# Cross-attention with a gate: the step without a tile gets an x half of the gate and two q pieces, the columns of q are cut anew, and the opening and the last steps are written in another order

## The chip, the cores and the metric

The kernel runs on one core of a Trainium2 chip. The metric is the device time of one execution in microseconds, the median of several runs. TensorE (PE in the rows) does the matmuls, VectorE (DVE), ScalarE (ACT) and GpSimd (POOL) the elementwise work, and SyncE (SP) hands out all the DMA transfers.

## What is computed

For 32 batches of 112 rows x (512 wide) with a memory of 375 keys (256 wide), in float32:

```python
memory_proj = einsum('bme,de->bmd', memory, W_mem)
scores = einsum('bnd,bmd->bnm', x, memory_proj) / sqrt(512)
attn = softmax(scores)
memory_context = einsum('bnm,bmd->bnd', attn, memory_proj)
gate = sigmoid(einsum('bnf,df->bnd', concat([x, memory_context]), W_gate) + b_gate)
fused = x + gate * memory_context
out = fused * rsqrt(mean(fused**2) + 1e-6) * norm_w
```

The kernel reorders this: q = x W_mem (256 wide) is multiplied with the memory itself, and `am`, the mean of the memory under the softmax, is multiplied with W_mem and with the gate weights.

## The kernel before

**Precision.** Each operand of a matmul is split into a high and a low part (`_hi`, `_lo`, type fp32r); a product is three kinds of matmul: high x high, high x low, low x high. ACT writes the high part as a copy, DVE or POOL the low part as a difference. So each product needs an ACT copy and a difference ahead of it.

**Tiling.** Eight batches are a group of 896 columns of x turned (`xT`), four groups in all. q of a group is computed in three units of columns (`UNITS`), and each unit in two halves of 128; one such piece (`q_piece(group, unit, half)`) is 12 matmuls with as many columns as the unit has. The gate works on tiles of 128 rows, seven to a group, 28 in all (`LAST` is 27).

**Steps.** After an opening written by hand, the program of each engine is a loop over steps; step s works on batch s. On PE a step is: `score(s)`, 6 matmuls of 376 columns; `gate_x(t + 2)`, the x half of a later tile's gate, 12 of 512; `attend(s - 1)`, 9 of 256; pieces of q, if the step has any (`q_pieces_at`); `gate_am(t)` and `context(t)`, 6 of 512 each, where t is the tile of the step (`tile_at`). Seven tiles go with eight batches, so in steps 10, 18 and 26 there is no tile: before, they hold only a score and an attend. The step after such a one (11, 19, 27) and step 3 open a group's tiles; below they are called "first-tile steps".

**What a step waits for.** `score(s)` needs q of its batch (`unit_of`) and both parts of the memory turned, `memT`, whose low part POOL makes one step ahead (`split_memT(s + 1)`, behind `inverse_rms` on POOL). `attend(s - 1)` needs the softmax of batch s - 1 turned (`pT`): DVE turns 32x32 blocks (`turn_p`), SP moves the blocks by four DMAs (`move_p`), ACT and DVE split the result (`pT_high`, `pT_low`). DVE goes strictly in its order, and there `pT_low(s - 1)` stands behind `maximum(s)`, `turn_p(s)` and `shares(s)`, that is, behind the softmax of the step's own batch. `am` goes the same way by `turn_am`, `move_am`, `amT_high`, `amT_low`, two steps later, to `gate_am`. `context(t)` writes a single bank, so it waits for `norm(t - 1)`. On DVE a tile runs through `add_bias`, `gate_context` (after ACT's `tanh`), `fuse`, and, after ACT's `square` and POOL's `inverse_rms`, `norm`.

**Queues.** SP hands out transfers in the order in which they are written and waits in that order: a transfer behind a wait for `turn_p` leaves no earlier than that. `load_mems(n)` brings both forms of a batch's memory, `load_xT` a unit of columns, `load_x` a tile of x.

The lines that the wait for the softmax and the tile's wait rest on:

```python
# DVE, one step
maximum(n); fuse(before); turn_p(n); shares(n)
pT_low(s - 1); amT_low(s - 2); norm(before); turn_am(s - 1)
# PE, context(t)
if bank is ctx_ps and t > 0:
    pe.wait_ge(y_ready, t)
```

## Time and profile before

| | us |
|---|---|
| median of three runs | 317.22 (317.0 to 317.82) |
| the profiled execution: time | 318.19 |
| the profiled execution: span of the trace | 316.4 |
| PE busy in it | 285.4 |

The time of the profiled execution lies 1.79 us over its span, and 0.97 us over the median. A row of the trace in order of time gives the start of a run of like instructions, its length, engine and line, output and inputs, shapes, how many they are, and in brackets the idle time of the engine ahead of it with what released it. Matmuls overlap, so the time that one costs is the distance of starts, not its length.

### The profile page before, as it was taken

What the parts mean: (1) busy time and instruction counts of PE and PEld (TensorE: products, weight loads), DVE (VectorE), ACT (ScalarE), POOL (GpSimd) and SP (SyncE); (2) the same over time, 40 slices, a digit from 0 to 9 for tenths busy, and PEclk for the clock granted to TensorE, in tenths of its full rate; (3) what the DMA queues carried; (4) which work ended last, traced back from release to release, by engine and by line L of the source; (5) the groups of instructions that cost most, each with busy time, mean ns of one, the idle gap of its engine ahead of it and who ended that gap; (6) DMA issues with size and microseconds to landing.
All of it is one profiled execution on the core that took longest, in us unless ns stands there. A gap on an engine that the chain in (4) does not pass through costs nothing. (4 is left out here: it accounts for less than half of the span.)

```text
span 316.4 us, 4881 instructions
## 1 busy us (share of the span) xinstructions
PE 285.4 (90%) x1479; PEld 245.8 (78%) x1479; DVE 183.8 (58%) x356; ACT 174.4 (55%) x363; POOL 190.3 (60%) x257
## 2 busy tenths in 40 slices
PE   8999599999999599999999599999999499997861
PEld 4988488878888498888888498888888498885651
DVE  4996337756665526766665436766655536666443
ACT  4874447556655626655655535655746545655321
POOL 1273537955949654965949653955958852674211
PEclk9999779999999799999999699999999899999987
DMA  7957965886955583796955684695956574563211
GB/s 278 420 174 229 301 222 148 254 238 200 281 155 137 174 261 115 220 275 178 293 161 132 183 258 119 190 282 168 262 158 179 192 202 120 133 183 98 82 41 67
DMA packets 52873, 61.41 MB, mean 194 GB/s; under 512 B 38640, under 2 KB 38896, under 8 KB 52592
## 3 DMA queue, kind: packets, MB, share of 16 engines
q1 hardware_dynamic: 52848, 61.10, 64.7%
q8 instruction: 12, 0.20, 0.3%
q14 instruction: 13, 0.11, 0.1%
HBM read 43.25 MB, written 7.34 MB: 160 GB/s over the span
## 5 line engine op out<-in xcount | busy, mean ns | idle before, releaser
L887 POOL TENSOR_TENSOR memT_lo<-mems_raw,memT_hi 128x376 fp32r<-128x376 f32 x42 | 41.9, 1016 | 29.5 <-ACT memT_hi L541 29.4
L887 POOL TENSOR_TENSOR mem_lo<-mems_raw,mem_hi 128x256 fp32r<-128x256 f32 x66 | 48.5, 763 | 11.8 <-ACT mem_hi L541 10.9
L912 POOL TENSOR_TENSOR guarded<-meansq,eps 128x1 f32<-128x1 f32 x27 | 11.8, 438 | 67.2 <-ACT work L598 67.1
L603 ACT ACTIVATE work<-work 128x512 f32<-128x512 f32 (+1 forms) x29 | 17.8, 617 | 34.4 <-DVE work L746 34.4
L574 ACT ACTIVATE probs<-score_ps,shift 112x375 f32<-112x375 f32 x32 | 18.3, 572 | 28.7 <-DVE shift L717 28.7
L351 PE MATMUL gate_ps<-wgx_hi,xT_hi 128*128 128x512 f32 x108 | 32.6, 428 | 0.0
L353 PE MATMUL gate_ps<-wgx_lo,xT_hi 128*128 128x512 f32 x108 | 31.1, 412 | 0.0
L589 ACT ACTIVATE am<-am_bank,share 112x256 f32<-112x256 f32 x32 | 15.2, 473 | 27.3 <-issue 27.0
L752 DVE SCALAR_TENSOR_TENSOR ctx_ps<-work,ctx_ps 128x512 f32<-128x512 f32 x27 | 18.8, 696 | 19.2 <-ACT work L603 18.3
L746 DVE TENSOR_TENSOR work<-gate_ps,b_gate 128x512 f32<-128x512 f32 (+1 forms) x29 | 19.4, 671 | 17.1 <-PE gate_ps L358 17.1
L358 PE MATMUL gate_ps<-wgx_hi,xT_lo 128*128 128x512 f32 x108 | 29.2, 393 | 0.0
L887 POOL TENSOR_TENSOR xT_lo<-xT_raw,xT_hi 128x320 fp32r<-128x320 f32 (+1 forms) x36 | 28.8, 832 | 0.0
L737 DVE STREAM_TRANSPOSE blocks_am<-am 128x256 f32<-128x256 f32 x32 | 14.2, 443 | 24.0 <-ACT am L589 24.0
L717 DVE TENSOR_REDUCE shift<-score_ps 112x1 f32<-112x375 f32 x32 | 17.5, 547 | 17.2 <-PE score_ps L358 17.2
L351 PE MATMUL score_ps<-memT_hi,qT_hi 128*112 128x376 f32 x64 | 17.4, 355 | 10.5 <-POOL memT_lo L887 10.5
L767 DVE SCALAR_TENSOR_TENSOR work<-ctx_ps,rstd,norm_w 128x512 f32<-128x512 f32 x27 | 20.3, 751 | 11.1 <-POOL rstd L914 11.1
L353 PEld LDWEIGHTS gate_ps<-wgx_lo,xT_hi 128*128 128x128 f32 x108 | 22.0, 204 | 5.4
L541 ACT ACTIVATE wgc_hi<-pT_raw 128x384 fp32r<-128x384 f32 x32 | 16.5, 516 | 17.5 <-DMA pT_raw<-blocks_p 17.5
L723 DVE STREAM_TRANSPOSE blocks_p<-probs 128x384 f32<-128x384 f32 x32 | 18.5, 578 | 11.0 <-ACT probs L574 8.5
L358 PEld LDWEIGHTS gate_ps<-wgx_hi,xT_lo 128*128 128x128 f32 x108 | 20.7, 192 | 4.6
L351 PEld LDWEIGHTS gate_ps<-wgx_hi,xT_hi 128*128 128x128 f32 x108 | 22.1, 209 | 2.8
L358 PE MATMUL am_bank<-mem_hi,wgc_hi 128*112 128x256 f32 x96 | 17.3, 289 | 7.0 <-DVE wgc_hi L704 7.0
(132 smaller groups left out, 712.7 us busy)
## 6 DMA issues: line engine op xcount, KB each, us to landing
mems_raw<-in_mems SPq DMA_DIRECT2D x20, 760.0 KB, 4.9
x_rows<-in_x SPq DMA_DIRECT2D x28, 256.0 KB, 5.5
out<-work SPq DMA_DIRECT2D x27, 256.0 KB, 5.8
first_raw<-in_mems SPq DMA_DIRECT2D x9, 760.0 KB, 5.0
pT_raw<-blocks_p SPq DMA_DIRECT2D x128, 48.0 KB, 2.8
xT_raw<-in_xT SPq DMA_DIRECT2D x7, 640.0 KB, 6.4
amT_raw<-blocks_am SPq DMA_DIRECT2D x128, 32.0 KB, 1.9
xT_raw<-in_xT SPq DMA_DIRECT2D x3, 512.0 KB, 6.2
```

Source lines behind the costliest of these rows:

```text
L351: pe.matmul(out, l_hi, r_hi, start=first and i == 0, stop=False)
L353: pe.matmul(out, l_hi, r_lo, start=False, stop=False)
L358: mm = pe.matmul(out, l_lo, r_hi, start=False, stop=last and i == len(lefts) - 1)
L541: return act.activation(out, in_, ACT.Copy)
L574: act.activation(probs[0:ROWS, 0:KEYS], scores[:, 0:KEYS], ACT.Exp, bias=shift[:, n % 2:n % 2 + 1], accum_out=total[:, n % 2:n % 2 + 1]).t ...
L603: act.activation(z[:, t % 2, cols], z[:, t % 2, cols], ACT.Tanh, scale=0.5).then_inc(tanh_ready, 1)
L717: dve.tensor_reduce(shift[:, s], scores[:, 0:KEYS], AX.X, ALU.max, negate=True).then_inc(shift_ready, 1)
L723: dve.transpose(turned_p[n % 2], probs_blocks).then_inc(blocks_p_ready, 1)
L746: dve.tensor_tensor(z[:, t % 2, cols], gate_ps[t % 3][:, cols], b_gate[:, cols], ALU.add).then_inc(z_ready, 1)
L752: dve.scalar_tensor_tensor(out=bank[:, cols], in0=z[:, t % 2, cols], scalar=1.0, in1=bank[:, cols], op0=ALU.add, op1=ALU.mult).then_inc(u_ ...
L767: dve.scalar_tensor_tensor(out=y[:, t % 2, cols], in0=bank[:, cols], scalar=rstd[:, t % 2:t % 2 + 1], in1=norm_w[:, cols], op0=ALU.mult, o ...
L887: return pool.tensor_tensor(out, in_, high.bitcast(F32), ALU.subtract)
```

## The change

The units of q become 336, 336 and 224 columns, which are 3, 3 and 2 whole batches. Both pieces of unit 1 go into the step without a tile, both pieces of unit 2 stay in the first-tile step, now in the first group as well. `gate_x` of a group's third tile moves from the first-tile step to the step ahead of it. The blocks of `am` get two buffers on both sides of their DMA. The opening's loads and splits are put in another order, the second half of the first load goes into `x_rows`, and the last steps are written out on every engine, with POOL's splits of the last two memories ahead of the tiles' `inverse_rms`, and the last x half cut in two.

```diff
-UNITS = [(0, 256), (256, 320), (576, 320)]
+UNITS = [(0, 336), (336, 336), (672, 224)]
...
-STEPS = BATCHES + TILE_LAG - 1
-OPENING = 3
+OPENING, ENDING = 3, BATCHES - 2
...
+def x_half_at(step):
+
+    group, of = divmod(step - TILE_LAG, GROUP)
+    return TILES * group + of + 2 if of > 0 else None
+
+
 def q_pieces_at(step):
     group, of = divmod(step, GROUP)
-    if of in (0, 1):
-        return [(group, 1, of)] if 1 <= group < GROUPS else []
+    if of == 2:
+        return [(group, 1, 0), (group, 1, 1)]
     if of == 3:
-        return [(group, 2, 0), (group, 2, 1)] if 1 <= group < GROUPS else []
+        return [(group, 2, 0), (group, 2, 1)]
     if of in (6, 7):
         return [(group + 1, 0, of - 6)] if group + 1 < GROUPS else []
...
-def softmaxes_at(step):
-
-    if step == BATCHES - 2:
-        return [step, step + 1]
-    return [step] if step < BATCHES - 2 else []
...
-        blocks_am = sb("blocks_am", [P, E])
-        amT_raw = sb("amT_raw", [P, E])
+        blocks_am = sb("blocks_am", [P, 2, E])
+        amT_raw = sb("amT_raw", [P, 2, E])
...
-        firsts = [first_raw[:, 0:FIRST], work[:, 4:6].rearrange("p s d -> p (s d)")]
+        firsts = [first_raw[:, 0:FIRST], x_rows[:].rearrange("p s d -> p (s d)")[:, 0:FIRST]]
...
-                if n >= 1:
-                    sp.wait_ge(amT_lo_ready, n)
+                if n >= 2:
+                    sp.wait_ge(amT_lo_ready, n - 1)
                 for q in range(Q):
-                    sp.dma_start(amT_flat[:, q], blocks_am_rows[q]).then_inc(am_turned, 16)
+                    sp.dma_start(amT_flat[n % 2][:, q], blocks_am_rows[n % 2][q]).then_inc(am_turned[n % 2], 16)
...
-            sp.dma_start(wgx_raw[:], wgT_d[:, 0:DC]).then_inc(wgx_loaded, 16)
             load_mem(0)
-            load_xT(0, 2)
-            sp.wait_ge(wm_hi_ready, 1)
-            sp.wait_ge(wm_lo_ready, 1)
+            sp.wait_ge(wm_hi_ready, 2)
+            sp.wait_ge(wm_lo_ready, 2)
             sp.wait_ge(x0_hi_ready, 1)
             sp.wait_ge(x0_lo_ready, 1)
+            sp.wait_ge(xT_hi_ready, 1)
+            sp.wait_ge(xT_lo_ready, 1)
+            sp.dma_start(wgx_raw[:], wgT_d[:, 0:DC]).then_inc(wgx_loaded, 16)
             load_memT(2)
+            load_xT(0, 2)
+            load_mem(1)
             move_p(0)
-            load_mem(1)
             sp.wait_ge(wgc_lo_ready, DC)
             sp.dma_start(wmT_raw, wmT_d).then_inc(wmT_loaded, 16)
+            load_mem(2)
+            load_mems(3)
             move_p(1)
             sp.dma_start(b_gate[:], b_d.partition_broadcast(P)).then_inc(vectors_loaded, 16)
             sp.dma_start(norm_w[:], nw_d.partition_broadcast(P)).then_inc(vectors_loaded, 16)
-            load_mem(2)
...
-            load_mems(3)
             move_p(2)
             sp.wait_ge(wgx_lo_ready, DC)
             for t in range(X_SLOTS):
                 load_x(t)
+            load_mems(4)
             load_xT(1, 0)
             move_am(1)
-            load_mems(4)
             load_mems(5)
...
-            for s in range(OPENING, STEPS):
-                for n in softmaxes_at(s)[:1]:
-                    move_p(n)
-                if s - 1 < BATCHES:
-                    move_am(s - 1)
-                for n in softmaxes_at(s)[1:]:
-                    move_p(n)
+            for s in range(OPENING, ENDING):
+                move_p(s)
+                move_am(s - 1)
                 if s + RAW < BATCHES:
                     load_mems(s + RAW)
                 if x_load_at(s) is not None:
                     load_xT(*x_load_at(s))
                 if tile_at(s - 1) is not None:
                     finish(tile_at(s - 1))
+            n = ENDING
+            move_p(n)
+            move_am(n - 1)
+            finish(LAST - 4)
+            move_p(n + 1)
+            move_am(n)
+            move_am(n + 1)
+            finish(LAST - 3)
+            finish(LAST - 2)
+            finish(LAST - 1)
...
-            def gate_x(t):
+            def gate_x(t, kinds=slice(0, 3)):
                 if t == 1:
                     pe.wait_ge(wga_lo_ready, 1)
                 if t >= 3:
                     pe.wait_ge(z_ready, t - 2)
                 c = t % TILES * P
-                product(gate_ps[t % 3][:],
-                        [(xT_hi[:, i, c:c + P], xT_lo[:, i, c:c + P]) for i in range(DC)],
-                        [(wgx_hi[:, i], wgx_lo[:, i]) for i in range(DC)], True, False).then_inc(gate_x_done, 1)
+                for left, right in ((xT_hi, wgx_hi), (xT_hi, wgx_lo), (xT_lo, wgx_hi))[kinds]:
+                    for i in range(DC):
+                        mm = pe.matmul(gate_ps[t % 3][:], left[:, i, c:c + P], right[:, i],
+                                       start=left is xT_hi and right is wgx_hi and i == 0, stop=False)
+                if kinds.stop == 3:
+                    mm.then_inc(gate_x_done, 1)
...
-            q_piece(0, 2, 0)
-            q_piece(0, 2, 1)
-
-            for s in range(OPENING, STEPS):
+            gate_x(2)
+
+            for s in range(OPENING, ENDING):
                 t = tile_at(s)
-                for n in softmaxes_at(s)[:1]:
-                    score(n)
-                if t is not None and t + 2 < LAST:
-                    gate_x(t + 2)
-                if s - 1 < BATCHES:
-                    attend(s - 1)
-                if s == BATCHES:
-                    gate_x(LAST)
-                for n in softmaxes_at(s)[1:]:
-                    score(n)
+                score(s)
+                if x_half_at(s) is not None:
+                    gate_x(x_half_at(s))
+                attend(s - 1)
                 for g, unit, half in q_pieces_at(s):
                     q_piece(g, unit, half)
                 if t is not None:
                     gate_am(t)
-                    if t < LAST:
-                        context(t)
+                    context(t)
+
+            n = ENDING
+            score(n)
+            gate_x(LAST - 1)
+            score(n + 1)
+            attend(n - 1)
+            gate_am(LAST - 3)
+            context(LAST - 3)
+            attend(n)
+            gate_x(LAST, slice(0, 2))
+            attend(n + 1)
+            gate_x(LAST, slice(2, 3))
+            for t in (LAST - 2, LAST - 1, LAST):
+                gate_am(t)
+                if t < LAST:
+                    context(t)
...
-            split_xT(0, 2)
             attended(0)
             split_mem(1)
+            split_memT(3)
             pT_high(1)
             exponentials(2)
+            split_xT(0, 2)
             wmT_high(0)
             wmT_high(1)
-            split_memT(3)
             attended(1)
+            split_mem(2)
             amT_high(0)
-            q_high(0, 2, 0)
-            split_mem(2)
-            q_high(0, 2, 1)
...
+            pT_high(n - 1)
+            split_memT(n + 1)
+            exponentials(n)
+            square(LAST - 4)
+            amT_high(n - 2)
+            exponentials(n + 1)
+            attended(n - 1)
+            split_mem(n)
+            split_mem(n + 1)
+            tanh(LAST - 3)
+            pT_high(n)
+            attended(n)
+            square(LAST - 3)
+            amT_high(n - 1)
+            pT_high(n + 1)
+            attended(n + 1)
+            tanh(LAST - 2)
+            amT_high(n)
+            square(LAST - 2)
+            tanh(LAST - 1)
+            amT_high(n + 1)
+            square(LAST - 1)
...
+            n = ENDING
+            gate_context(LAST - 4)
+            maximum(n)
+            fuse(LAST - 4)
+            turn_p(n)
+            shares(n)
+            pT_low(n - 1)
+            amT_low(n - 2)
+            maximum(n + 1)
+            norm(LAST - 4)
+            turn_am(n - 1)
+            turn_p(n + 1)
+            shares(n + 1)
+            add_bias(LAST - 3)
+            pT_low(n)
+            gate_context(LAST - 3)
+            turn_am(n)
+            fuse(LAST - 3)
+            amT_low(n - 1)
+            pT_low(n + 1)
+            norm(LAST - 3)
+            turn_am(n + 1)
+            add_bias(LAST - 2)
+            gate_context(LAST - 2)
+            amT_low(n)
+            fuse(LAST - 2)
+            add_bias(LAST - 1)
+            norm(LAST - 2)
+            amT_low(n + 1)
+            gate_context(LAST - 1)
+            fuse(LAST - 1)
...
+            split_memT(ENDING + 1)
+            inverse_rms(LAST - 4)
+            split_mem(ENDING)
+            split_mem(ENDING + 1)
+            for t in (LAST - 3, LAST - 2, LAST - 1):
+                inverse_rms(t)
```

In the rows of PE, score_ps is a score, am_bank an attend, gate_ps with wgx an x half of the gate and with wga its am half, ctx_ps a context and q_ps a piece of q. PE before, in the two steps around which the group turns: the attend of step 10, which has no tile, and then all of step 11 up to its pieces of q.

```order
L351 MATMUL am_bank<-mem_hi,wgc_hi 112x256 x3
L353 MATMUL am_bank<-mem_lo,wgc_hi 112x256 x3
L358 MATMUL am_bank<-mem_hi,wgc_hi 112x256 x3
L351 MATMUL score_ps<-memT_hi,qT_hi 112x376 x2
L353 MATMUL score_ps<-memT_lo,qT_hi 112x376 x2
L358 MATMUL score_ps<-memT_hi,qT_lo 112x376 x2
L351 MATMUL gate_ps<-wgx_hi,xT_hi 128x512 x4
L353 MATMUL gate_ps<-wgx_lo,xT_hi 128x512 x4
L358 MATMUL gate_ps<-wgx_hi,xT_lo 128x512 x4
L351 MATMUL am_bank<-mem_hi,wgc_hi 112x256 x3
L353 MATMUL am_bank<-mem_lo,wgc_hi 112x256 x3
L358 MATMUL am_bank<-mem_hi,wgc_hi 112x256 x3
```


In the changed kernel, from the x half that step 10 has now, through attend and both pieces of q of unit 1, to the score of step 11:

```order
L430 MATMUL gate_ps<-wgx_hi,xT_hi 128x512 x4
L430 MATMUL gate_ps<-wgx_lo,xT_hi 128x512 x4
L430 MATMUL gate_ps<-wgx_hi,xT_lo 128x512 x4
L358 MATMUL am_bank<-mem_hi,wgc_hi 112x256 x3
L360 MATMUL am_bank<-mem_lo,wgc_hi 112x256 x3
L365 MATMUL am_bank<-mem_hi,wgc_hi 112x256 x3
L358 MATMUL q_ps<-xT_hi,wm_hi 128x336 x4
L360 MATMUL q_ps<-xT_lo,wm_hi 128x336 x4
L365 MATMUL q_ps<-xT_hi,wm_lo 128x336 x4
L358 MATMUL q_ps<-xT_hi,wm_hi 128x336 x4
L360 MATMUL q_ps<-xT_lo,wm_hi 128x336 x4
L365 MATMUL q_ps<-xT_hi,wm_lo 128x336 x4
```


And step 11 of the changed kernel, from its score to its pieces of q:

```order
L358 MATMUL score_ps<-memT_hi,qT_hi 112x376 x2
L360 MATMUL score_ps<-memT_lo,qT_hi 112x376 x2
L365 MATMUL score_ps<-memT_hi,qT_lo 112x376 x2
L358 MATMUL am_bank<-mem_hi,wgc_hi 112x256 x3
L360 MATMUL am_bank<-mem_lo,wgc_hi 112x256 x3
L365 MATMUL am_bank<-mem_hi,wgc_hi 112x256 x3
L358 MATMUL q_ps<-xT_hi,wm_hi 128x224 x4
L360 MATMUL q_ps<-xT_lo,wm_hi 128x224 x4
L365 MATMUL q_ps<-xT_hi,wm_lo 128x224 x4
L358 MATMUL q_ps<-xT_hi,wm_hi 128x224 x4
L360 MATMUL q_ps<-xT_lo,wm_hi 128x224 x4
L365 MATMUL q_ps<-xT_hi,wm_lo 128x224 x4
```


So the x half of four matmuls three times stands between score and attend in step 10 and no longer in step 11, the pieces of unit 1 have come into step 10, and the score of step 11 stands right behind the two pieces of q that it needs.

SP in the opening before, from the move of batch 0's softmax to the load of the second group's x (mems_raw and first_raw take the memories, 1520 columns are a whole batch):

```order
L270 DMA pT_raw<-blocks_p 128x1x96 x4
L258 DMA mems_raw<-in_mems 128x768
L309 DMA work<-in_wmT 128x1024
L270 DMA pT_raw<-blocks_p 128x1x96 x4
L311 DMA b_gate<-in_b 128x512
L312 DMA norm_w<-in_nw 128x512
L258 DMA first_raw<-in_mems 128x768
L277 DMA amT_raw<-blocks_am 128x1x64 x4
L263 DMA mems_raw<-in_mems 128x1520
L270 DMA pT_raw<-blocks_p 128x1x96 x4
L280 DMA x_rows<-in_x 128x512 x4
L251 DMA xT_raw<-in_xT 128x1024
```


SP there in the changed kernel:

```order
L269 DMA pT_raw<-blocks_p 128x1x96 x4
L310 DMA work<-in_wmT 128x1024
L257 DMA first_raw<-in_mems 128x768
L262 DMA mems_raw<-in_mems 128x1520
L269 DMA pT_raw<-blocks_p 128x1x96 x4
L314 DMA b_gate<-in_b 128x512
L315 DMA norm_w<-in_nw 128x512
L276 DMA amT_raw<-blocks_am 128x1x64 x4
L269 DMA pT_raw<-blocks_p 128x1x96 x4
L279 DMA x_rows<-in_x 128x512 x4
L262 DMA mems_raw<-in_mems 128x1520
L250 DMA xT_raw<-in_xT 128x1344
```


The load of batch 3's memory (the first of 1520 columns) now stands ahead of the second move of pT instead of behind the first move of am, and that of batch 4 ahead of the load of xT.

PE at the end before, from the second score of step 30 on:

```order
L351 MATMUL score_ps<-memT_hi,qT_hi 112x376 x2
L353 MATMUL score_ps<-memT_lo,qT_hi 112x376 x2
L358 MATMUL score_ps<-memT_hi,qT_lo 112x376 x2
L351 MATMUL gate_ps<-wga_hi,amT_hi 128x512 x2
L353 MATMUL gate_ps<-wga_lo,amT_hi 128x512 x2
L358 MATMUL gate_ps<-wga_hi,amT_lo 128x512 x2
L351 MATMUL ctx_ps<-wmT_hi,amT_hi 128x512 x2
L353 MATMUL ctx_ps<-wmT_lo,amT_hi 128x512 x2
L358 MATMUL ctx_ps<-wmT_hi,amT_lo 128x512 x2
L351 MATMUL am_bank<-mem_hi,wgc_hi 112x256 x3
L353 MATMUL am_bank<-mem_lo,wgc_hi 112x256 x3
L358 MATMUL am_bank<-mem_hi,wgc_hi 112x256 x3
```


PE at the end in the changed kernel, from the attend behind the context of tile 24 on:

```order
L358 MATMUL am_bank<-mem_hi,wgc_hi 112x256 x3
L360 MATMUL am_bank<-mem_lo,wgc_hi 112x256 x3
L365 MATMUL am_bank<-mem_hi,wgc_hi 112x256 x3
L430 MATMUL gate_ps<-wgx_hi,xT_hi 128x512 x4
L430 MATMUL gate_ps<-wgx_lo,xT_hi 128x512 x4
L358 MATMUL am_bank<-mem_hi,wgc_hi 112x256 x3
L360 MATMUL am_bank<-mem_lo,wgc_hi 112x256 x3
L365 MATMUL am_bank<-mem_hi,wgc_hi 112x256 x3
L430 MATMUL gate_ps<-wgx_hi,xT_lo 128x512 x4
L358 MATMUL gate_ps<-wga_hi,amT_hi 128x512 x2
L360 MATMUL gate_ps<-wga_lo,amT_hi 128x512 x2
L365 MATMUL gate_ps<-wga_hi,amT_lo 128x512 x2
```


So an attend follows each context, the x half of tile 27 stands around the last attend, and the am halves of tiles 25, 26 and 27 come after all of it.

## Rows read from the trace of the kernel before

**Rows 1.** Waits of PE: us in total, times, longest us.

```profile
PE score_ps L351 <- POOL memT_lo L887: 10.5, 5, 3.5
PE am_bank L358 <- DVE wgc_hi L704: 7.0, 6, 1.7
```

**Rows 2.** PE in order of time, steps 10 to 12: start, us, idle before.

```profile
100.14 0.51 PE L351 MATMUL score_ps<-memT_hi,qT_hi 128*112 128x376 f32 x2
103.79 0.60 PE L358 MATMUL am_bank<-mem_hi,wgc_hi 128*112 128x256 f32 x3 [1.74 <-DVE wgc_hi L704]
106.62 0.57 PE L351 MATMUL score_ps<-memT_hi,qT_hi 128*112 128x376 f32 x2 [2.23 <-POOL memT_lo L887]
...
112.06 0.51 PE L351 MATMUL am_bank<-mem_hi,wgc_hi 128*112 128x256 f32 x3
...
113.09 0.74 PE L351 MATMUL q_ps<-xT_hi,wm_hi 128*128 128x320 f32 x4
...
116.60 0.63 PE L351 MATMUL gate_ps<-wga_hi,amT_hi 128*128 128x512 f32 x2
...
119.40 0.50 PE L351 MATMUL score_ps<-memT_hi,qT_hi 128*112 128x376 f32 x2
...
120.44 1.08 PE L351 MATMUL gate_ps<-wgx_hi,xT_hi 128*128 128x512 f32 x4
...
123.17 0.52 PE L351 MATMUL am_bank<-mem_hi,wgc_hi 128*112 128x256 f32 x3
```

**Rows 3.** Windows: length, busy of PE, PEld, DVE, ACT, POOL, granted clock, DMA share, GB/s.

```profile
100.14:119.40 19.26, 15.30 (x79) 13.42 (x78) 8.46 (x18) 8.98 (x20) 11.58 (x15) 0.91 0.74 214
171.67:191.46 19.79, 15.84 (x80) 13.96 (x79) 8.46 (x18) 8.88 (x20) 11.81 (x15) 0.83 0.72 207
244.21:263.54 19.33, 15.33 (x80) 13.55 (x79) 8.45 (x18) 8.88 (x20) 11.81 (x15) 0.91 0.67 183
178.15:184.00 5.85, 5.85 (x18) 5.01 (x19) 1.97 (x5) 2.21 (x5) 3.09 (x5) 0.61 0.59 173
287.00:296.50 9.50, 6.53 (x33) 4.53 (x32) 6.16 (x11) 5.05 (x12) 5.29 (x9) 1.00 0.40 109
```

**Rows 4.** DVE in order of time, step 10: the low part of pT.

```profile
103.20 0.53 DVE L704 TENSOR_TENSOR wgc_hi<-pT_raw,wgc_hi 128x384 fp32r<-128x384 f32 x1
```

**Rows 5.** ACT in order of time, step 11: a copy of q after its piece.

```profile
116.80 0.44 ACT L567 ACTIVATE qT_hi<-q_ps 128x320 fp32r<-128x320 f32 x1 [1.32 <-PE q_ps L358]
```

**Rows 6.** Groups of PE and of its weight loads (PEld), shapes apart: busy us, mean ns.

```profile
L358 PE MATMUL q_ps<-xT_hi,wm_lo 128*128 128x256 f32 x24 | 3.9, 283 | 0.0
...
L358 PEld LDWEIGHTS q_ps<-xT_hi,wm_lo 128*128 128x128 f32 x84 | 12.7, 189 | 0.0
```

**Rows 7.** The opening in order of time: PE, ACT and POOL up to step 4.

```profile
36.74 0.94 PE L351 MATMUL score_ps<-memT_hi,qT_hi 128*112 128x376 f32 x2 [3.52 <-POOL memT_lo L887]
...
47.18 0.50 PE L351 MATMUL score_ps<-memT_hi,qT_hi 128*112 128x376 f32 x2
...
33.44 0.83 ACT L541 ACTIVATE memT_hi<-mems_raw 128x752 fp32r<-128x752 f32 x1 [5.10 <-DMA mems_raw<-in_mems]
...
41.09 0.42 ACT L541 ACTIVATE amT_hi<-amT_raw 128x256 fp32r<-128x256 f32 x1 [0.87 <-DMA amT_raw<-blocks_am]
...
44.40 1.95 POOL L887 TENSOR_TENSOR memT_lo<-mems_raw,memT_hi 128x376 fp32r<-128x376 f32 x2 [5.86 <-ACT memT_hi L541]
```

**Rows 8.** The end in order of time: PE step 30, DVE, and one tile on DVE.

```profile
278.75 0.51 PE L351 MATMUL score_ps<-memT_hi,qT_hi 128*112 128x376 f32 x2
...
307.54 0.76 DVE L746 TENSOR_TENSOR work<-gate_ps,b_gate 128x256 f32<-128x256 f32 x2 [2.23 <-PE gate_ps L358]
...
46.04 0.69 DVE L746 TENSOR_TENSOR work<-gate_ps,b_gate 128x512 f32<-128x512 f32 x1 [0.46 <-PE gate_ps L358]
...
51.66 0.75 DVE L767 SCALAR_TENSOR_TENSOR work<-ctx_ps,rstd,norm_w 128x512 f32<-128x512 f32 x1 [0.44 <-POOL rstd L914]
```

**Rows 9.** PE in order of time, step 6: a wait that recurs in each group.

```profile
67.70 0.61 PE L358 MATMUL am_bank<-mem_hi,wgc_hi 128*112 128x256 f32 x3 [0.63 <-DVE wgc_hi L704]
```

More of the change, by code:

```diff
@@ L692, in _ @@
                     split_xT(*x_unit_at(s))
-                if t is not None and t < LAST:
+                if t is not None:
                     tanh(t)
+            n = ENDING
[21 more added lines that the diff above has]
+            square(LAST - 1)
             for i, cols in enumerate(HALVES):
@@ L829, in _ @@
             wga_low(1)
-            c, n = UNITS[2]
-            dve.wait_ge(xT_hi_ready, 3)
-            low(xT_lo[:, :, c:c + n], raw_of(2), xT_hi[:, :, c:c + n]).then_inc(xT_lo_ready, 1)
             turn_am(0)
@@ L837, in _ @@
             shares(2)
+            c, n = UNITS[2]
+            dve.wait_ge(xT_hi_ready, 3)
+            low(xT_lo[:, :, c:c + n], raw_of(2), xT_hi[:, :, c:c + n]).then_inc(xT_lo_ready, 1)
             wmT_low(0)
@@ L841, in _ @@
             amT_low(0)
-            q_low(0, 2, 0)
-            q_low(0, 2, 1)
-            for s in range(OPENING, STEPS):
+            for s in range(OPENING, ENDING):
                 t, before = tile_at(s), tile_at(s - 1)
@@ L925, in _ @@
             split_mem(2)
-            for s in range(OPENING, STEPS):
-                before, late = tile_at(s - 1), softmaxes_at(s)[1:]
-                if late:
-                    split_memT(s + 1)
+            for s in range(OPENING, ENDING):
+                before = tile_at(s - 1)
                 if before is not None:
                     inverse_rms(before)
-                if s + 1 < BATCHES and not late:
-                    split_memT(s + 1)
-                if s < BATCHES:
-                    split_mem(s)
+                split_memT(s + 1)
+                split_mem(s)
                 if x_unit_at(s) is not None:
                     split_xT(*x_unit_at(s))
+            split_memT(ENDING + 1)
[4 more added lines that the diff above has]
+                inverse_rms(t)
             a, b = slice(2, 3), slice(3, 4)
```

75 lines of the change are left out of this document (28 added, 47 removed).

## The prediction, made before the changed kernel ran

> **What bounds the kernel now.** I read the table first: PE is busy 285.4 of 316.4 us, so PE's own work is the floor and the question is where PE stands still. The view of waits names two places [rows 1]: scores that wait for POOL's low part of the memory (10.5 us, five times) and attends whose last third waits for the low part of pT (7.0 us, six times). PE's order in time shows where both fall: in the step without a tile and the one after it. In step 10 the score starts at 100.14, and the last third of attend(9) only at 103.79, after 1.74 us of idling; then the score of step 11 idles 2.23 us more [rows 2]. From score(10) to score(12) 19.26 us pass, in the other two groups 19.79 and 19.33 [rows 3]. The work in it, from starts where PE runs freely [rows 2]: a score 1.04 (119.40 to 120.44), an x half 2.73 (120.44 to 123.17), an attend 1.03 (112.06 to 113.09), two pieces of q 3.51 (113.09 to 116.60), am half with context 2.80 (116.60 to 119.40). Two scores, two attends and one of each other make 13.18. So 6.08, 6.61 and 6.15 are lost, **18.84 us in three groups**. About 4 of each is idle time; the rest is the clock, which falls after it: 0.61 of full speed in the 5.85 us from 178.15 on, which hold one score and one x half, 3.77 us of work [rows 3]. The opening has such a place too, a score that idles 3.52 us because the memory of batch 3 came late: ACT waited 5.10 us for that load [rows 7].
>
> **The middle: three groups.** The step without a tile gets an x half between score and attend. In steps that have one the wait for pT is covered (none at 123.17 [rows 2]), so it goes there. Both pieces of unit 1 make the step longer by 3.7 us more, which is time for POOL: the 2.23 us go too. But the x half is taken from the first-tile step, and the wait for pT goes with the missing x half. From the first matmul of a score to the last third of the attend behind it 3.65 us pass (100.14 to 103.79 [rows 2]), because DVE does the low part of pT only at 103.20 [rows 4], behind maximum and turning of the step's own softmax. With score (1.04) and two thirds of attend (0.69) in between, 1.92 us stay lost. Late next is q: score(11) now stands right behind the pieces of unit 1, which it needs. After a piece ACT starts its copy 0.20 after PE's next start and takes 0.44 (116.60, 116.80 [rows 2, 5]); with 0.06 for the signal (my allowance) PE loses 0.70. The low part follows on DVE under the score's first four matmuls. First-tile steps thus lose 2.62 us, three times 7.86.
>
> **The pieces of q.** The 24 matmuls of a group's unit 0 go from 256 to 336 columns, those of unit 1 from 320 to 336, those of unit 2 from 320 to 224. A matmul of 320 costs 3.51 / 24 = 0.1463, one of 512 costs 2.73 / 12 = 0.2275; on that line 336 cost 0.1531. No matmul of this type in the trace has fewer than 256 columns. Below: the line gives 0.1057 for 224. Above: a piece that overlapped with nothing would take its weight load and its matmul, 0.189 + 0.283 = 0.472 [rows 6]. I take the nearest row, 256 columns in attend, 1.03 / 9 = 0.114, as if nothing were gained below 256. Then a group costs 24 x (2 x 0.1531 + 0.114 - 0.114 - 2 x 0.1463) = 0.33 more, 1.0 in three.
>
> The Trainium skill bears on this ("TensorE: Matmul & The Clock Gate", section on LDWEIGHTS): a weight load takes its columns divided by 1.2 GHz, 107 ns for 128, whatever the matmul behind it. By that rule 224 columns can't run on the line to 0.1057, but at 0.107 to 0.114; the sum would be up to 96 x 0.007 = 0.7 us better than mine. No run here shows a piece short enough to tell.
>
> **What else rides on the groups.** In steps 6, 14 and 22 the last third of attend waits a little, 0.63 in step 6 [rows 9], for a pT that lands behind a unit of columns. That unit and POOL's split of it grow by a twentieth to a third; I add 0.25 each, 0.75 (bounds 0 and 0.8 each). The two buffers of am take away waits that stand on no path of PE in the middle: 0. Middle: -18.84 + 7.86 + 1.0 + 0.75 = **-9.2**.
>
> **The opening.** Batch 3's load leaves SP ahead of two moves, so score(3) no longer waits for it; its place takes the wait for pT, 1.92. PE alone would gain 3.52 + 2.1 (clock, taken as 5.85 - 3.77 above) - 1.92 - 0.33 (pieces) = 3.4. But the move of am(1) still stands behind four x tiles, and now behind batch 4's load as well, so I leave its copy on ACT at 41.09 (0.42); behind it come batch 4's copy (0.83, as at 33.44) and POOL's split (1.95) [rows 7]. score(4) then starts at 44.3 and not 47.18: **-2.9**, with bounds of -1.5 (first load a sixth larger) and -4.5.
>
> **The end.** From score(30) at 278.75 to the first add_bias of the last tile at 307.54 are 28.79 us [rows 8]. The work is two scores, three attends, two x halves, four am halves and three contexts: 2.08 + 3.09 + 5.46 + 9.8 = 20.4, so 8.4 are lost. Written out, PE waits as I follow the orders: 0.9 for POOL's split of memory 30, 1.6 for pT(31), which stands on ACT behind square(24), 0.6 for am(30), and about 2.7 for context(26). The last is the largest: context(26) needs norm(25), and from a tile's add_bias to the end of its norm 6.37 us pass (46.04 to 52.41 [rows 8]), some 5.8 without the maximum between, while PE has only context(25), the am half of 26 and the 0.6 to do. With 0.2 to the add_bias: 26.4, **-2.4** (bounds -1 and -3.5). What follows stays as it is.
>
> **Sum.** -9.2 - 2.9 - 2.4 = -14.5. The profiled execution took 318.19, so 303.7 for it; it stood 0.97 over the median, which gives **302.7**.
>
> **Rivals.**
> *The clock falls all the same.* The lost time moves rather than goes: 0.7 and 1.92 us of idling lie within 5 us. Against it: between 287.0 and 296.5 PE was busy 6.53 of 9.50 us and the clock stayed at 1.00 [rows 3]. For it: the falls at 178.15 followed waits of 4 us that were no single one. Price 2.1 a time, three times: 309.
> *Short pieces are dear.* If below 256 columns loads and matmuls cease to overlap, 96 matmuls (24 in each of four groups, all in PE's path) cost up to 0.472 - 0.114 more each, 34 us: 337, slower. It decides from 14.5 / 96 = 0.15 more each, that is 0.265 a matmul. For it: every matmul of this type in the trace has at least 256 columns. Against it: from 512 down to 256 the cost lies on one line without a step.
> *Shorter steps run into POOL and SP.* Steps 8 and 9 lose their piece of q. If the wait of step 6 came twice as long and in more steps, 0.8 to 2 a group: 305 to 308.
> *The wait only moves.* If the first-tile step lost what step 10 loses now, clock included, the middle would give nothing, the units would cost 1.8 and opening and end would give 5.3: 313.7, still faster.
>
> **How the numbers follow.** Forecast 0.62, its own range 297 to 308 from the bounds of the terms. Clock 0.15, shorter steps 0.07, wait only moved 0.02: faster as well, together 0.86. Short pieces 0.12, slower. No change within 0.3% (about what a measurement tells): 0.02. The range leaves out the short pieces and little else: 297 to 312.
>
> **What would show it.** After the change, PE: no wait in step 10; in step 11 a score that starts 0.7 after the last piece and a last third of attend that waits about 1.7; granted clock 1.00 through both; from score(4) to score(12) 69 us (now 72.2); pieces of 224 at 0.114 or less; score(4) at 44. Wrong it would be made above all by pieces of 224 above 0.2, by a clock at half speed in steps 11, 19 and 27, or by waits in step 8 or 9 that are not there now.

## The result, and the profile after

The changed kernel takes 317.74 us (median of 20 executions), the kernel before 318.66 in the same series: ratio 0.9948, 95% interval 0.9925 to 0.9971. It is faster by half a per cent at most, where 15 us were forecast. The ratios here and below leave out executions more than 1.5% slower than the fastest of the same kernel, so a ratio is not the quotient of the two medians. The profiled execution took 318.57 us, its span is 316.8 (before 316.4).

The forecast cut the kernel into three stretches, and so does the comparison, by starts of scores (before: [rows 2, 7, 8]):

| stretch | before | forecast | after |
| --- | --- | --- | --- |
| to score(4) | 47.18 | -2.9 | 50.38, **+3.2** |
| score(4) to score(28) | 216.36 | -9.2 | 209.81, **-6.55** |
| score(30) to the end of the span | 37.65 | -2.4 | 41.37, **+3.7** |

So the middle gained two thirds of what it should, and the opening and the end lost more than they should have gained. The waits of PE in the changed kernel, largest first (engine, tile, line, who it waits for: us in total, times, longest):

```profile
PE am_bank L365 <- DVE wgc_hi L733: 5.8, 4, 1.8
PE gate_ps L358 <- ACT amT_hi L559: 5.5, 2, 4.9
PE am_bank L358 <- ACT wgc_hi L559: 4.1, 2, 3.1
PE ctx_ps L358 <- DVE work L796: 2.8, 4, 2.1
PE am_bank L358 <- POOL mem_lo L936: 2.0, 2, 1.0
PE score_ps L358 <- ACT qT_hi L585: 1.6, 3, 0.5
```

Against [rows 1] the scores' 10.5 us for POOL are gone (0.8 stay). New are one wait of 4.95 us of an am half for its copy on ACT and one of 3.1 us of an attend for pT's.

**The opening.** The order of PE in time has both sides of the first (start, duration, instruction, idle time before it and its releaser):

```profile
40.53 0.61 PE L365 MATMUL q_ps<-xT_hi,wm_lo 128*128 128x224 f32 x4
46.09 1.19 PE L358 MATMUL gate_ps<-wga_hi,amT_hi 128*128 128x512 f32 x2 [4.95 <-ACT amT_hi L559]
...
50.38 0.51 PE L358 MATMUL score_ps<-memT_hi,qT_hi 128*112 128x376 f32 x2
```

Behind the wait the am half and the context take 4.29 us instead of the 2.80 of [rows 2]: the clock fell here, too. ACT was not busy with something else; it waited for the transfer:

```profile
45.53 0.42 ACT L559 ACTIVATE amT_hi<-amT_raw 128x256 fp32r<-128x256 f32 x1 [8.83 <-DMA amT_raw<-blocks_am]
```

SP's queue shows when that transfer, am(1)'s move, was handed out, and behind what:

```profile
31.45 2.48 SPq L269 DMA_DIRECT2D pT_raw<-blocks_p  x4
33.98 2.01 SPq L279 DMA_DIRECT2D x_rows<-in_x  x4
36.09 0.38 SPq L262 DMA_DIRECT2D mems_raw<-in_mems  x1
36.51 0.43 SPq L250 DMA_DIRECT2D xT_raw<-in_xT  x1
36.98 3.83 SPq L276 DMA_DIRECT2D amT_raw<-blocks_am  x4
```

A move of four DMAs of 32 KB (am) or 48 KB (p) takes SP 2.48 us or more, most loads of 760 KB 0.34 to 0.54. Ahead of am(1) stand four x tiles (1 MB), batch 4 (0.78 MB, new in this place) and xT (0.69 MB). [Rows 7] had the copy at 41.09.

**The middle.** Step 11, the first-tile step of the first group:

```profile
108.21 0.78 PE L365 MATMUL q_ps<-xT_hi,wm_lo 128*128 128x336 f32 x4
109.53 0.60 PE L358 MATMUL score_ps<-memT_hi,qT_hi 128*112 128x376 f32 x2 [0.54 <-ACT qT_hi L585]
...
113.26 0.61 PE L365 MATMUL am_bank<-mem_hi,wgc_hi 128*112 128x256 f32 x3 [1.75 <-DVE wgc_hi L733]
113.71 0.68 PE L358 MATMUL q_ps<-xT_hi,wm_hi 128*128 128x224 f32 x4
114.19 1.05 PE L360 MATMUL q_ps<-xT_lo,wm_hi 128*128 128x224 f32 x4
```

These are the two waits of the forecast, in steps 11, 19 and 27 alike. The brackets give idle time; the forecast counted distances of starts, and by these the waits cost what it said. A row of four matmuls of 336 columns takes 0.61, so the score comes 0.71 late (0.70 forecast), and from the score to attend's last third 3.73 us pass, 2.00 more than the work (1.92 forecast). But the pieces behind them go from 0.44 to 0.85 us a row: the clock. In the windows from attend's last third to the next score (busy time of PE, PEld, DVE, ACT, POOL, then the granted clock, DMA share, GB/s) the same work takes 1.6 us more in two of three; without these two falls the middle would have gained 9.8 (9.2 forecast):

```profile
113.26:120.81 7.55, 7.55 (x39) 7.00 (x40) 2.20 (x5) 2.32 (x5) 4.15 (x5) 0.77 0.84 254
183.71:189.63 5.92, 5.92 (x39) 5.36 (x40) 2.19 (x5) 2.33 (x5) 4.19 (x5) 1.00 0.75 234
252.66:260.19 7.53, 7.53 (x39) 7.00 (x40) 2.21 (x5) 2.31 (x5) 4.17 (x5) 0.77 0.58 156
```

Two smaller things changed beside it. The waits of steps 6, 14 and 22 [rows 9], which the forecast let grow, are all but gone: these steps took 9.95, 9.25 and 9.74 us and now take 9.51, 9.51 and 9.69 with longer pieces of q, against the 9.03 and 9.47 of a step 7 without a wait, 1.5 us less of waiting in all. Instead the context of steps 5, 13 and 21 waits a little for the norm of the tile before; these steps take 8.06 to 8.08 us instead of 7.61, 1.4 in all:

```profile
64.61 0.70 PE L358 MATMUL ctx_ps<-wmT_hi,amT_hi 128*128 128x512 f32 x2 [0.21 <-DVE work L796]
```

**The end.** The forecast's four waits are there: 0.99 for memory 30, 0.52 for am(30), 2.13 for context(26) (0.9, 0.6 and 2.7 said), and in place of 1.6 for pT(31) the 3.09 below. A fifth, 0.57 of score(31) for POOL, was not forecast.

```profile
292.31 0.98 PE L358 MATMUL am_bank<-mem_hi,wgc_hi 128*112 128x256 f32 x3 [3.09 <-ACT wgc_hi L559]
293.09 0.84 PE L360 MATMUL am_bank<-mem_lo,wgc_hi 128*112 128x256 f32 x3
```

ACT again waits for a transfer (1.70 us, copy at 291.73), which SP hands out 3.2 us after DVE has turned p(31) (283.84), because am(29)'s move and a finish stand ahead:

```profile
283.40 2.48 SPq L276 DMA_DIRECT2D amT_raw<-blocks_am  x4
285.93 0.59 SPq L279 DMA_DIRECT2D x_rows<-in_x  x1
286.56 0.43 SPq L286 DMA_DIRECT2D out<-work  x1
287.09 3.22 SPq L269 DMA_DIRECT2D pT_raw<-blocks_p  x4
```

```profile
291.73 0.52 ACT L559 ACTIVATE wgc_hi<-pT_raw 128x384 fp32r<-128x384 f32 x1 [1.70 <-DMA pT_raw<-blocks_p]
```

Behind it the clock is 0.60 from 292 to 300 us, and it falls once more behind the wait for context(26). The first line is that place up to the last tile's first add_bias; the second is the same work, behind the same wait, in the experiment with a single am buffer, where the clock did not fall (columns as above):

```profile
304.37:309.06 4.69, 4.69 (x15) 3.73 (x16) 1.58 (x3) 0.69 (x2) 0.09 (x1) 0.64 0.15 56
300.54:303.70 3.16, 3.16 (x15) 2.62 (x16) 1.73 (x3) 0.42 (x1) 0.00 (x0) 1.00 0.50 176
```

So from score(30) to that add_bias 33.63 us pass (275.43 to 309.06; 28.79 before, 26.4 forecast).

**How far a single time can be trusted.** Executions of the changed kernel lie between 310.9 and 321.1 us over two series, with mean clocks from 0.959 to 0.992. Where an effect is under 3 us, read the stretch of the trace that the edit touches.

### The profile page after: what moved, and what is told of

Read it like the earlier page. It is cut to its first block and busy times, and to the rows that moved or that the text cites. A ratio compares the mean times of both kernels' runs of the same rounds, so it can differ in the third digit from the quotient of the medians.

```text
span 316.8 us, 4880 instructions
## 1 busy us (share of the span) xinstructions
PE 286.3 (90%) x1479; PEld 245.7 (78%) x1479; DVE 186.8 (59%) x356; ACT 172.8 (55%) x363; POOL 191.3 (60%) x257
## 5 line engine op out<-in xcount | busy, mean ns | idle before, releaser
L936 POOL TENSOR_TENSOR mem_lo<-mems_raw,mem_hi 128x256 fp32r<-128x256 f32 x66 | 48.6, 763 | 7.0 <-ACT mem_hi L559 6.0
L936 POOL TENSOR_TENSOR xT_lo<-xT_raw,xT_hi 128x336 fp32r<-128x336 f32 (+1 forms) x36 | 29.8, 862 | 0.2
L430 PE MATMUL gate_ps<-wgx_hi,xT_hi 128*128 128x512 f32 x108 | 29.4, 394 | 0.0
L430 PE MATMUL gate_ps<-wgx_lo,xT_hi 128*128 128x512 f32 x108 | 29.1, 391 | 0.0
L739 DVE SCALAR_TENSOR_TENSOR qT_lo<-q_ps,qT_hi 128x336 fp32r<-128x336 f32 (+1 forms) x22 | 10.1, 465 | 24.3 <-ACT qT_hi L585 24.1
L358 PE MATMUL gate_ps<-wga_hi,amT_hi 128*128 128x512 f32 x56 | 19.1, 424 | 5.5 <-ACT amT_hi L559 5.5
L430 PEld LDWEIGHTS gate_ps<-wgx_lo,xT_hi 128*128 128x128 f32 x108 | 20.3, 188 | 4.7
L733 DVE TENSOR_TENSOR wgc_hi<-pT_raw,wgc_hi 128x384 fp32r<-128x384 f32 x32 | 19.9, 623 | 6.5 <-ACT wgc_hi L559 6.5
L936 POOL TENSOR_TENSOR memT_lo<-first_raw,memT_hi 128x376 fp32r<-128x376 f32 x20 | 20.7, 1056 | 4.3 <-ACT memT_hi L559 4.3
```

The source lines that it names most:

```text
L358: pe.matmul(out, l_hi, r_hi, start=first and i == 0, stop=False)
L430: mm = pe.matmul(gate_ps[t % 3][:], left[:, i, c:c + P], right[:, i], start=left is xT_hi and right is wgx_hi and i == 0, stop=False)
L733: return dve.tensor_tensor(out, in_, high.bitcast(F32), ALU.subtract)
L936: return pool.tensor_tensor(out, in_, high.bitcast(F32), ALU.subtract)
```

## The experiments

The theory: three separate causes. In the opening am(1)'s place in SP's queue, at the end p(31)'s, in the middle a wait that takes the clock with it. The main rival: the same bytes must land in any order, so waits only move.

**The opening: am(1) and batch 4 ahead of the x tiles.**

```diff
             move_p(2)
+            load_mems(4)
+            move_am(1)
             sp.wait_ge(wgx_lo_ready, DC)
             for t in range(X_SLOTS):
                 load_x(t)
-            load_mems(4)
             load_xT(1, 0)
-            move_am(1)
```

> The changed kernel with one edit in SP's opening: the loads of batch 4 and the move of am(1) stand ahead of the four x tiles and of xT instead of behind them. Theory A (am(1)'s move stands in SP's queue behind 2.5 MB of other loads, and the gate's am half of tile 0 waits for its copy 4.95 us): amT_hi(1) is copied by about 41 us instead of 45.53, the gate's am half has no wait left, TensorE keeps its clock there, score(4) starts at 43.8 to 44.5 us instead of 50.38, and the kernel takes about 6 us less (311 to 312 us). Rival B (it is the bytes that must land, in whatever order): the copies are only late elsewhere, at the x tiles or xT, score(4) stays at 48 us or later, and the time within 2 us of the changed kernel's 317.7.

312.94 us, ratio to before 0.9808 (0.9775 to 0.9840). amT_hi(1) was copied at 39.77 us, the am half waited for nothing, score(4) started at 43.81: the place in the queue set it, as theory A says. The time is 4.8 us less than the changed kernel's, not the 6 expected: of the 6.6 us only 3.3 were left at score(6) (62.75 for 66.08), since the next move now stood behind the x tiles; on SP, and what ACT saw of it:

```profile
34.66 2.48 SPq L276 DMA_DIRECT2D amT_raw<-blocks_am  x4
37.19 2.02 SPq L279 DMA_DIRECT2D x_rows<-in_x  x4
...
40.26 2.88 SPq L269 DMA_DIRECT2D pT_raw<-blocks_p  x4
```

```profile
48.60 0.52 ACT L559 ACTIVATE wgc_hi<-pT_raw 128x384 fp32r<-128x384 f32 x1 [4.36 <-DMA pT_raw<-blocks_p]
```

**From the changed kernel again, only batch 4 back behind am(1)**, the order of before there: `load_xT(1, 0)`, `move_am(1)`, `load_mems(4)`, `load_mems(5)`.

> The changed kernel with the order xT, am(1), batch 4, batch 5 of the kernel before in SP's opening, so that only the 0.78 MB of batch 4 no longer stand ahead of am(1). Theory A (the queue's order): amT_hi(1) is copied some 2 us earlier than 45.53, at about 43.3, score(4) starts at about 47.5 instead of 50.38, and the kernel takes 2.5 to 2.9 us less; if batch 4 then comes late, memT_lo(4) shows it as the wait before score(4). Rival B (bytes, not order): score(4) stays within 0.7 us of 50.38 and the time within 1 us.

313.70 us, 0.9846 (0.9812 to 0.9880). amT_hi(1) came at 43.84 as expected:

```profile
43.84 0.42 ACT L559 ACTIVATE amT_hi<-amT_raw 128x256 fp32r<-128x256 f32 x1 [5.07 <-DMA amT_raw<-blocks_am]
```

So the load of batch 4 accounts for 1.7 of the 4.4 us by which the copy was late; the other 2.75 stay with the order of before. There SP hands out p(2) at 32.23 us and am(1) at 37.28 (29.59 and 35.71 before), and the copy starts 4.1 us after the end of that handing out instead of 2.9. Batch 4 was now late in its turn (its copy at 45.97, after 1.71 us of waiting), and score(4) came at 49.09: 1.3 us gained, between the two expectations. The rest of the 4 us does not lie where the edit does: in this trace score(4) to score(28) takes 207.3 us (209.8 in the changed kernel), with the clock falling in none of steps 11, 19 and 27, and the end 37.9 (41.4).

**Then p(3), too, ahead of most x tiles** (one x tile, p(3), batch 5, am(2), then the rest).

> The opening's edits alone: batch 4 and am(1), then one x tile, p(3), batch 5, am(2), then the other x tiles and xT. Theory (place in SP's queue): score(4) at 43.5 to 44.5 us as with the first edit, score(5) at 51.3 to 52.3 instead of 54.08, and 7.5 to 8.5 us less than the changed kernel up to score(6), if nothing is late behind. Rival: xT or an x tile, now last, is late in step 4 or 5 and takes 2 us back.

310.94 us, 0.9741 (0.9702 to 0.9780). score(4) 44.56, score(5) 52.17 as expected, but score(6) at 61.76, 4.3 us earlier and not 8: attend(4) now waits 0.37 and 1.10 us in step 5. Each move put first makes the next one late, so here the rival holds in part.

**The end: p(31) first.**

```diff
             move_p(n)
-            move_am(n - 1)
             finish(LAST - 4)
             move_p(n + 1)
+            move_am(n - 1)
             move_am(n)
```

with pT(31)'s copies ahead of `square(LAST - 3)` and am(29)'s on ACT, and ahead of am(29)'s on DVE.

> The changed kernel with the end reordered: SP moves p(31) ahead of am(29) and am(30), and ACT and DVE copy pT(31) ahead of amT(29). Theory A (each move of four DMAs holds SP some 2.5 us, and p(31)'s move stood behind am(29)'s): attend(31) starts at about 289 us instead of 292.31, its wait of 3.09 us is gone, TensorE's clock does not fall to 0.51 there, and the kernel takes 4 to 5 us less. Rival B (the wait only moves): am(29) is then late, the gate's am half of tile 25 waits 2 us or more in place of attend(31), and the time stays within 1 us.

312.55 us, 0.9807 (0.9771 to 0.9844). SP hands out p(31) at 283.29, attend(31) runs at 288.50 without a wait, am(29) is not late, the clock stays at 1.00 to 300 us, and the end takes 34.14 us instead of 41.37. What is left there is the wait for context(26):

```profile
288.50 0.52 PE L358 MATMUL am_bank<-mem_hi,wgc_hi 128*112 128x256 f32 x3
...
297.71 0.71 PE L358 MATMUL ctx_ps<-wmT_hi,amT_hi 128*128 128x512 f32 x2 [2.14 <-DVE work L796]
```

**The end in the order of before**, on all engines; units and am buffers as changed.

> The changed kernel with the last three steps in the order of the kernel before on all engines; the units of 336, 336 and 224 columns, the step's x half and the two am buffers stay. Theory A (the written-out end lost 3.7 us: 41.37 us from score(30) to the end of the span where it was 37.65): the end takes 37.5 to 38 us again and the kernel 3.5 us less. Rival B (the end is longer for what the loop leaves to it, whatever its order): it stays above 40 us and the time within 1 us.

313.62 us, 0.9806 (0.9765 to 0.9847). The end takes 37.4 us, as before. Ten traces, with those of the experiments below, hold the end as changed: 37.0, 37.7, 37.9 and 38.5 us in four, 40.3 to 41.4 in six, with a wait of 2.4 to 4.0 for pT(31) in each. What parts the six from the four is the fall of the clock behind the wait for context(26): from there to the last tile's first add_bias they take 4.64 to 4.69 us, the four 3.16. Behind attend(31) it fell in the six as well, and in one of the four (38.5). So the new order is at best 0.6 us better than the old one (37.65 and 37.4), and mostly 3 us worse.

**The middle: pieces of q between the scores and attend in first-tile steps.**

```diff
+                if s % GROUP == TILE_LAG:
+                    for g, unit, half in q_pieces_at(s):
+                        q_piece(g, unit, half)
                 attend(s - 1)
-                for g, unit, half in q_pieces_at(s):
-                    q_piece(g, unit, half)
+                if s % GROUP != TILE_LAG:
+                    for g, unit, half in q_pieces_at(s):
+                        q_piece(g, unit, half)
```

> The changed kernel with one edit on TensorE: in the steps of a first tile the pieces of q stand between the step's scores and attend instead of behind attend. Theory A (attend's second part waits 1.75 us for pT's low part, and where the clock falls after it that costs another 1.65 us): the wait is gone in steps 11, 19 and 27, the clock stays at 1.00, the stretches from score(4) to score(12), score(20) and score(28) take 68.7, 67.1 and 68.7 us at most instead of 70.43, 68.82 and 70.56, and the kernel about 7 to 9 us less. Rival B (what comes behind attend on ACT and DVE is then late in its turn, turn_am and the next am): the wait moves to the gate's am half or to the context of the same step, and the time stays within 2 us.

310.45 us, 0.9746 (0.9692 to 0.9801). Steps 11, 19 and 27 have only the 0.54 ahead of their scores left; attend runs through:

```profile
114.72 0.50 PE L360 MATMUL am_bank<-mem_lo,wgc_hi 128*112 128x256 f32 x3
115.06 0.50 PE L365 MATMUL am_bank<-mem_hi,wgc_hi 128*112 128x256 f32 x3
```

The three groups take 67.66, 66.91 and 66.97 us, 8.3 less together. Theory A, to its numbers.

**The same in steps without a tile**, there with q's copies ahead of attend's on ACT and DVE.

> The same edit, and in the steps without a tile too, with q's copies ahead of attend's on ACT and DVE there. Theory A: besides what the edit in the first-tile steps gives, the wait of 0.54 us before the scores of steps 11, 19 and 27 (for q's copy on ACT) is gone, some 2 us less than that kernel. Rival B: q's copies ahead of attend's delay am, and the gate's am half of the step behind waits as long as is gained: within 0.7 us of that kernel.

317.93 us, 0.9960 (0.9922 to 0.9998): not better by 2 but worse by 7.5 than the edit before; neither expectation. The 0.54 is gone (0.46 for am comes in its place, in step 11), but am(9) is turned 3.9 us later (110.89 for 106.96), its move comes later on SP, and p(11), behind it and the loads, is handed out later:

```profile
111.36 2.48 SPq L276 DMA_DIRECT2D amT_raw<-blocks_am  x4
...
116.25 2.80 SPq L269 DMA_DIRECT2D pT_raw<-blocks_p  x4
```

```profile
125.23 0.61 PE L358 MATMUL am_bank<-mem_hi,wgc_hi 128*112 128x256 f32 x3 [2.54 <-ACT wgc_hi L563]
```

In the kernel of the edit before, SP hands out am(9) at 107.43 and p(11) at 113.79.

**The wait filled with useless work**, to see the clock alone:

```diff
                 high_lefts(am_ps, turned, memory)
+                if fill is not None:
+                    for _ in range(11):
+                        pe.matmul(q_ps[fill][:, 0:336], wm_hi[:, 0, 0:P], xT_hi[:, 0, 0:336], start=True, stop=True)
                 pe.wait_ge(pT_lo_ready, n + 1)
```

> The changed kernel with 11 more matmuls of 336 columns (1.69 us by their rows) between attend's two parts in steps 11, 19 and 27, whose output is overwritten: they put work into the wait of 1.75 us for pT's low part and bring no result. Clock theory (the granted clock falls because TensorE idles there): the clock is 1.00 behind attend in all three, steps 11 and 27 (7.50 us from attend's second part to the next scores) take 5.9 us as step 19 does, and the kernel 3.3 us less. Rival (the clock falls for what stands elsewhere, or what is behind attend waits for other engines anyway): no change, or the matmuls' own time on top, up to 0.3 us for each.

312.83 us, 0.9835 (0.9792 to 0.9878). Steps 11, 19 and 27 take 9.63, 9.66 and 9.65 us. By itself one trace proves little: in the nine traces that keep the bare wait these steps take 9.63 to 9.67 us from score to score in 16 cases and 11.26 to 11.29 in 11, in no fixed pattern (none of three in two of the traces). Where the wait is filled or gone (seven traces here, 21 steps) none fell.

**All edits at once.**

> The edits of the opening (batch 4 and am(1) ahead of the x tiles), of the end (p(31) ahead of am(29)) and of the middle (pieces ahead of attend in steps with a first tile and without a tile) in one kernel. If the three causes are separate, as the theory has it, the gains add: 6 + 4 to 5 + 9 to 11 us less than the changed kernel's 317.7, 296 to 300 us. If they share a cause (the transfers or the clock as a whole), it stays above 304.

311.53 us, 0.9799 (0.9757 to 0.9840): the gains did not add, because the edit in steps without a tile takes 12.8 and 12.5 us in steps 12 and 20 here too. So without it:

> The edits of the opening (batch 4 and am(1) ahead of the x tiles), of the end (p(31) ahead of am(29)) and of the first-tile steps alone (pieces of q ahead of attend; the steps without a tile stay as in the changed kernel). Each alone moved its own stretch of the trace: the start of score(6) 3.3 us earlier, the way from score(4) to score(28) 8.3 us shorter, the end 2.9 us of wait and up to 4 us of clock. Theory (three separate places): they add, a span of 298 to 302.5 us, 300 to 304 us of time. Rival (they share a limit, as the kernel with all edits, which took 311.5, may show): 308 us or more.

**301.45 us, 0.9467 (0.9432 to 0.9502).** score(4) 43.06, score(4) to score(28) 204.00, the end 34.62. They add. (That this comes near the 302.7 forecast for the change is chance: the waits that the forecast kept in first-tile steps are gone here, and waits in step 4 that it did not have are new.) With p(3) ahead as well:

> The same kernel, and in the opening p(3)'s move ahead of three of the four x tiles, of xT and of batch 5. Theory (after the opening's first edit the same thing happens one move on: p(3)'s move is handed out at 40.26 us behind x tiles and xT, its copy waits till 48.60, attend(3) idles 1.44 and 0.73 us and the clock falls in step 4): pT(3) is copied before 45 us, step 4 takes 7.6 to 8.1 us instead of 10.27, and the kernel 2 to 2.5 us less than the one with three edits. Rival (the bytes on the way decide): pT(3) still lands at 47 us or later, within 0.7 us.

301.49 us, 0.9466 (0.9423 to 0.9509). Step 4 takes 7.67 us, as expected, and step 5 10.13 instead of 8.64: attend(4) waits 1.18 and 0.83 us. The wait moved one step on. (The expectation has the clock fall in step 4 after the first edit; in that trace it was 1.00 from 46 to 58 us, and the step's 2.7 us over 7.61 are its two waits alone.)

**The am buffer.** The waits of a single buffer put back (SP's move waits for the low part before it, DVE's turning for the move before it).

> The changed kernel with the waits of a single am buffer put back: am's move waits until the low part of the am before it is taken, and the next turning until the move has landed. By the forecast (the second buffer takes away waits that stand on no path of TensorE in the middle): score(4) to score(28) within 0.7 us of 209.8, the whole within 1 us of 317.7 but for the end. Rival (the second buffer matters at the end, where am(30) and am(31) are moved in one go at 290.41): the end is 1.5 to 4 us longer, and the kernel as much slower.

314.44 us, 0.9869 (0.9824 to 0.9914), 3 us less than the changed kernel, though its waits are the same to 1.3 us: score(4) to score(28) takes 208.45 with one fall of the clock instead of two, the end 37.0. So both ran again, side by side.

> The changed kernel unchanged, once more, beside the two kernels below on one chip. If the second am buffer itself costs time (317.74 with it, 314.44 with the waits of one buffer put back), it takes 316.5 to 319 us again and the kernel with the waits of one buffer 3 us less. If the difference is that of the clock's falls from one execution and one chip to the next (mean clock 0.960 to 0.976 in the runs of the changed kernel, 0.970 to 0.982 in those with one buffer's waits), both take the same here within 1 us. In its trace the clock falls again in some of steps 11, 19 and 27, not in the same ones.

> The kernel with the waits of a single am buffer once more, beside the changed kernel. By the theory of the clock's falls: within 1 us of it; if the second buffer costs time: 2 to 4 us less than it.

317.44 and 317.24 us (before: 319.33). Side by side nothing is left of the 3 us, so the second buffer is not shown to cost or to give anything there; a difference under a microsecond would not show among executions that lie up to 10 us apart. In the trace of the first run the clock fell once instead of twice in the middle, and at neither of the two places at the end. In the three-edit kernel, however:

> The kernel with the three edits (301.45 us) with the waits of a single am buffer put back. By the forecast's zero for the second buffer, in the middle: score(4) to score(28) takes 204.0 us as with two buffers (within 0.7), and the whole is within 1.5 us of 301.45. If the second buffer costs time, 2 to 4 us less; if the shorter steps now need it (am's move then waits for the copy before it), 2 us more or above.

308.25 us, 0.9643 (0.9603 to 0.9682): 6.8 us slower than with two buffers. score(4) to score(28) takes 207.4 (204.0), the end 40.6 (34.6). Of the 3.4 in the middle 2.7 lie in step 4, which takes 12.5 us with two buffers as well (all edits at once), so they need not be the buffer's. At the end SP hands out the last three of am's moves over 17 us (9.0 with two buffers), since each waits for the copies of the one before:

```profile
276.80 17.01 SPq L276 DMA_DIRECT2D amT_raw<-blocks_am  x12
```

## Why the prediction was wrong, step by step

- **Opening, the failed step:** "so I leave its copy on ACT at 41.09". It came at 45.53. The same sentence had seen batch 4's load in front of it and put no price on it; the experiment with batch 4 behind am(1) gives 1.7 us. The other 2.75 us of delay remain without that load, where SP hands out everything from p(2) on 1.6 to 2.6 us later than before and the unit of xT in front is a third larger; which of the two weighs more was not tested. The wait of 4.95 us and 1.5 of clock behind it put score(4) at 50.38. With am(1) ahead of all of it, score(4) came at 43.81, which is the forecast for PE alone (3.4 us before 47.18); but only the next step had it, since p(3) was late in turn.
- **End, the failed step:** "1.6 for pT(31), which stands on ACT behind square(24)". I followed PE, ACT and DVE and gave SP no time. The wait was 3.09, for a transfer that SP handed out 3.2 us late. The forecast counted the work at full clock; the clock fell twice, which cost 2.8 us behind attend(31) (8.29 us to the am half of tile 26, 5.5 where it did not fall) and 1.5 behind the wait for context(26). Idle time was 7.3 in place of 5.8, and the work, with what each wait costs beyond its idle time, 1.4 more than the 20.4 forecast: together the 33.63 for 26.4. What follows did not stay as it is, but is 1.15 shorter (7.72 for 8.87). With p(31) first, 26.30 us pass (274.56 to 300.86). That this meets the 26.4 is luck: the wait of 1.6 for pT(31) in that sum is not there, and 0.88 for score(31) and 1.1 of work that were not in it are.
- **Middle, waits right, the failed step is the clock:** by distances of starts the two waits measured 2.71 a group (2.62 forecast). What failed is the argument that kept the clock out of the sum, "the clock stayed at 1.00" between 287.0 and 296.5 [rows 3]: that was one execution, and told nothing of how often. The clock rival, given 0.15, happened in part: 1.6 us where the clock falls (price 2.1), in 2 of 3 groups here and 11 of 27 in all. "I add 0.25 each" in steps 6, 14 and 22 had the wrong sign, -1.5 and not +0.75, and the 1.4 of waits for norms in steps 5, 13 and 21 were not foreseen; that the two cancel is luck. With 8.1 of waits, 3.3 for two falls, 0.8 for the units, 1.4 and -1.5 the sum from -18.84 is -6.7, for the measured -6.55.
- **Units of columns, right:** rows of four matmuls of 224 start every 0.445 us, 0.111 each (0.114 forecast), and 336 columns take 0.153 (0.1531). The short-piece rival is out. The Trainium skill's rule ("TensorE: Matmul & The Clock Gate", LDWEIGHTS) gives 107 ns for the weight load alone. The trace agrees as far as the pieces go, whose matmuls start 4 ns further apart than that; the load itself can't be read from it, since its rows are 0.19 us long and overlap.
- **The am buffers at 0:** right as far as the runs can tell in this kernel; that other waits cover theirs here is inferred. In the three-edit kernel, where those are gone, a single buffer costs 6.8 us, 6.0 of them at the end.
- **"Shorter steps run into POOL and SP"** was a rival of 0.07, looked for in steps 8 and 9. SP was the right engine, in the wrong places: the opening and the end.

Shown by experiment: the opening's and the end's order on SP, the wait in first-tile steps, and that the three add to 301.45. Open: why the clock falls after the same wait in one execution and not in the next, and what makes up the 2.75 us of the opening that are not batch 4's.

## What to carry to other kernels

The engine that hands out transfers has a timeline of its own: here a move of four DMAs held it 2.5 us, so whatever an edit puts ahead of such a move must be charged to the consumer of that move, bulk loads by their bytes as well. A wait of PE can be filled with PE's own next work: two pieces of q moved ahead of one attend in each of three groups took out 8.3 us of wait and clock, but the same edit one step earlier delayed a move and lost 7.5. An edit whose wait is covered by another measures as nothing until the cover is gone, so an edit like the second buffer is tried again in the improved kernel. And idle time in brackets is less than what a wait costs: here 0.54 and 1.75 us of idling moved the starts by 0.71 and 1.91, so a forecast by starts is compared with starts.

## What the runs showed of the hardware

- The clock fell after idle times of 0.54 and 1.75 us with 2.0 us of work between them in 11 of 27 like places, at 1.6 us each, and not at the same ones in two executions of one program. Rows of matmuls then took twice as long (0.44 to 0.85 us).
- Behind the wait of 2.13 us for context(26) it fell in 8 of the 15 traces that have it, at 1.5 us each.
- The time from the end of SP's handing out to the copy was longer where more had been handed out just before: 5.5 us for p(3), four DMAs of 48 KB behind x tiles, xT and memory (43.1 to 48.6), 1.5 us for p(2) ahead of them (33.98 to 35.44), both with ACT waiting for the transfer.
